# Edge scans set one at a time between a sort's comparisons, and a node search that only counts the keys below

## What is computed

```
edge_index = stack([src, dst]); x = layernorm(x + L0(x, edge_weight)); x = layernorm(x + L1(x, edge_attr_64)) ...
L0: col = dst;  geo_agg = x + segment_sum(w * x[col], col) / segment_sum(w, col);  two matmuls with relu
L1: agg_sum = segment_sum(edge_attr, dst); agg_max = segment_max(edge_attr, dst); cnt = segment_sum(1, dst)
    h = gelu([x, agg_sum, agg_max, agg_mean, u[batch]] @ W1 + b1) @ W2 + b2; layernorm; + x
L2: h = relu([x[src], x[dst]] @ W1 + b1); inter = h @ W2 + b2; gated = inter * sigmoid(inter @ Wg + bg)
    pooled = segment_sum(gated, src) / max(segment_sum(1, src), 1)
L3: attention over the edges of each dst (segment max, exp, segment sums of x[src] * alpha)
```

## Time and profile before

| | us |
|---|---|
| median of 3 runs (lowest, highest) | 5547.71 (5546.32, 5547.77) |
| the profiled execution: its time | 5548.05 |
| its span in the trace | 5546.3 |
| sort stage: scans on the DVE (388 full ones) | 476.2 |
| sort stage: comparisons and signs on the DVE | 420.7 |

### The profile page before, as it was taken

One profiled execution on the slowest core, in us unless ns is written; L12 is line 12 of the kernel. 1 busy time (PEld: TensorE's weight loads), 2 busy tenths in 40 slices (PEclk: granted clock), 3 DMA queues, 4 the chain that ended last, 5 costly groups with the idle time before them and its releaser, 6 DMA issues. The chain is left out here.

```text
span 5546.3 us, 56323 instructions
## 1 busy us (share of the span) xinstructions
PE 3195.1 (58%) x11758; PEld 1912.6 (34%) x11758; DVE 3739.0 (67%) x4499; ACT 1742.1 (31%) x3305; POOL 3549.1 (64%) x3650
## 2 busy tenths in 40 slices
PE   4666766274555555555555542666666676666661
PEld 2444444132333333333333322333333343333330
DVE  8998988683333333333333343888888888888886
ACT  2334444162111111111111111444444444444441
POOL 5244000656777777777777767777777777777773
PEclk8667777586777777777677765777777777777775
DMA  8876665463444444444444422444444444444441
GB/s 185 208 230 194 219 189 160 133 135 96 118 119 119 119 119 119 116 116 119 118 119 119 119 68 60 100 104 103 104 103 104 104 104 103 104 104 104 103 93 31
DMA packets 995252, 677.18 MB, mean 122 GB/s; under 512 B 645759, under 2 KB 799123, under 8 KB 994258
## 3 DMA queue, kind: packets, MB, share of 16 engines
q1 hardware_dynamic: 719604, 344.35, 25.3%
q0 software_dynamic: 116160, 120.60, 12.2%
q10 hardware_dynamic: 159390, 211.24, 10.7%
HBM read 343.26 MB, written 332.55 MB: 122 GB/s over the span
## 5 line engine op out<-in xcount | busy, mean ns | idle before, releaser
L1570 POOL DMA_INDIRECT got<-tabg,ix x1568 | 1479.3, 943 | 489.1 <-issue 477.6
L1763 POOL DMA_INDIRECT got<-tabg,ix x1568 | 1479.4, 943 | 477.7 <-issue 477.7
L177 PE MATMUL p_got<-ident,got 128*128 128x128 f32 (+1 forms) x784 | 208.0, 417 | 910.5 <-DMA got<-tabg,ix 910.5
L1684 DVE TENSOR_TENSOR pre<-own,p_got 128x512 f32<-128x512 f32 x196 | 134.4, 686 | 877.7 <-PE p_got L177 794.3
L184 PEld LDWEIGHTS p_out<-ident,run 128*128 128x128 f32 (+1 forms) x3136 | 532.1, 215 | 311.8 <-issue 304.2
L184 PE MATMUL p_out<-ident,run 128*128 128x128 f32 (+1 forms) x3136 | 625.0, 347 | 5.4 <-DVE run L1948 3.5
L1796 PE MATMUL p_got<-ident,got 128*128 128x128 f32 (+1 forms) x784 | 177.3, 366 | 654.0 <-DMA got<-tabg,ix 654.0
L1637 ACT ACTIVATE hid<-pre,B 128x512 f32<-128x512 f32 x196 | 141.2, 720 | 1278.7 <-DVE pre L1684 1278.7
L532 DVE TENSOR_TENSOR_SCAN run<-p_mk,run,feat 128x512 f32<-128x512 f32 x390 | 477.2, 1266 | 79.1 <-ACT feat L637 42.9
L177 PEld LDWEIGHTS p_got<-ident,got 128*128 128x128 f32 (+1 forms) x784 | 133.3, 208 | 958.9 <-DMA got<-tabg,ix 958.9
L1668 DVE TENSOR_TENSOR_SCAN own<-mk,own,p_first 128x512 f32<-128x512 bf16 x195 | 248.6, 1275 | 298.9 <-PE p_first L177 298.9
(11 more groups left out here) (358 smaller groups left out, 6641.9 us busy)
## 6 DMA issues: line engine op xcount, KB each, us to landing
t<-rows ACTq DMA_DIRECT2D x195, 512.0 KB
first<-start SPq DMA_DIRECT2D x390, 256.0 KB
t<-rows ACTq DMA_DIRECT2D x195, 288.0 KB, 2.3
got<-tabg,ix POOLq DMA_INDIRECT x3136
start<-zeros SPq DMA_DIRECT2D x100, 500.0 KB
ea<-in_ea_dram SPq DMA_DIRECT2D x390, 128.0 KB
mk<-marks SPq DMA_DIRECT2D x780, 64.0 KB, 2.7
start<-zeros SPq DMA_DIRECT2D x195, 256.0 KB
```

The lines of the kernel that those rows point to most:

```text
L177: mm = nc.tensor.transpose(by_place(bank, g)[:, :, cc], by_edges[0:g.p, cc, :, :].rearrange("p h f -> p (h f)"), ident[0:g.p, 0:g.p])
L1570: nc.gpsimd.indirect_dma_start(got[s][0:g.p, cc, h, :], None, tabg, bass.IndirectOffsetOnAxis(ap=ix[0:g.p, g.n, h, cc:cc + 1], axis=0)).th ...
L1763: nc.gpsimd.indirect_dma_start(got[s][0:g.p, cc, h, :], None, tabg, bass.IndirectOffsetOnAxis(ap=ix[0:g.p, g.n, h, cc:cc + 1], axis=0)).th ...
```

## The change

1. **Placement.** `scans_beside` counts 392 single scans. A scan comes after single comparison instructions, in proportion to their columns (1.14 scans per 1024 columns); a turn takes four scans, and before these one more where needed so that they begin with a sum (5 of the 12 turns that still have scans). The scans left when the last 32 steps begin, eight of them, all stand after the first instruction of that stretch.
2. **PE and ACT.** Work goes in entries, one per scan. An entry m (group n, kind) on the PE is: one mark matmul for that kind, waiting only for the scan of the same kind of group n-1; `p_out` of that scan; in a sum's entry also `p_in` of group n+1. In a turn the third entry stands between the second and third quarter of the keys. The marks have a semaphore per kind. All is written out, without loops.
3. **Search.** `count_keys` makes only the keys below; `has` and `first` are made once for all 49 columns by `find`, in tick 17, from `upto` (the next node's `before`). The carried column is issued by SP ahead of the table stores, and the scatter waits for `find`.

```
 def scans_beside(steps):
-    rate = (NG + 1 - 2 * turns) / (last - turns)
...
-        if what[0] == "turn":
-            k = 2
...
+    rate, credit, at, out = (SCANS - (IN_TURN + 1) * turns) / work, 0.0, 0, []
...
+        if i >= busy:
+            out.append([take(SCANS)])
+        elif what[0] == "turn":
+            out.append([take(at % 2), take(IN_TURN)])
+        else:
+            n, w = ops_of(what)
...
+            for _ in range(n):
+                credit += rate * w
...
 SP load
-                    wait_from(sp, spread, g.n - AHEAD + 1)
+                    wait_from(sp, marked_maxima, g.n - AHEAD + 1)
 DVE scan
-                    dve.wait_ge(spread, g.n + 1)
-                    dve.wait_ge(feats, g.n + 1)
-                    wait_from(dve, rowed, 2 * g.n - 2)
+                    dve.wait_ge(spread[kind], g.n + 1)
+                    if kind == 0:
+                        dve.wait_ge(feats, g.n + 1)
+                    wait_from(dve, rowed, m - 3)
 PE
+                def spread_marks(g, kind):
+                    wait_from(pe, scanned[kind], g.n)
+                    nc.tensor.matmul(p_mk[kind][:, 0:g.w], sel2[:, :], mk[g.slot(AHEAD)][:, kind, 0:g.w], start=True, stop=True).then_inc(spread[kind], 1)
+                def entry(m):
+                    n, kind = m // 2, m % 2
...
+                        spread_marks(Group(None, n), kind)
+                    if n > 0:
+                        turn_back(Group(None, n - 1), kind)
+                    if kind == 0 and n + 1 <= NG:
+                        turn_group(Group(None, n + 1))
 turn_keys
                     for q in range(4):
+                        if q == 2 and m < SCANS + 2:
+                            entry(m)
+                            m += 1
 ACT entry
+                    if kind == 1 and n + 1 <= NG:
+                        to_order(Group(None, n + 1))
+                    if n > 0:
+                        to_rows(Group(None, n - 1), kind)
 count_keys
-        nc.vector.tensor_tensor(self.upto_it[:, 0:k, :], keys, node, ALU.is_le).then_inc(self.v, 1)
...
+        self.link(dve, nc.vector.tensor_tensor(self.less[:, 0:k, :], keys, node, ALU.is_lt))
+        self.link(dve, nc.vector.tensor_reduce(self.count1[:, s], self.less[:, 0:k, :], AX.X, ALU.add))
+        nc.vector.scalar_tensor_tensor(out=self.before[:, s], in0=self.row[:, s], scalar=float(SORTED_KEYS), in1=self.count1[:, s],
+                                       op0=ALU.mult, op1=ALU.add).then_inc(self.counted, 1)
 SP of node_chain
+                if firsts_of:
+                    firsts_of.shift(sp)
                 for u, (a, k) in enumerate(UNITS):
...
-                if firsts_of:
-                    firsts_of.shift(sp)
 POOL of node_chain
-                        pool.wait_ge(firsts_of.found, u + 1)
+                        pool.wait_ge(firsts_of.found, 1)
```

More of the change, by code:

```diff
@@ L391, in mark_rows, with ops_of, take @@
     yield slice(E // SF, E // SF + 1), slice(0, E % SF), marks[1, kind, E // SF * SF - H:H].rearrange("(o f) -> o f", o=1)
-def scans_beside(steps):
-    last = len(steps) - QUIET
-    turns = sum(1 for what in steps[:last] if what[0] == "turn")
-    rate = (NG + 1 - 2 * turns) / (last - turns)
-    out, n, credit = [], 0, 0.0
+SCANS = 2 * (NG + 1)
+IN_TURN = 4
+def ops_of(what):
+    if what[0] == "sign":
+        return 1, SF // 2
+    return (4, SF // 4) if what[1] < ROW else (2, SF // 2)
+def scans_beside(steps):
+    busy = len(steps) - QUIET
+    turns = sum(1 for what in steps[:busy] if what[0] == "turn")
+    work = sum(n * w for n, w in (ops_of(what) for what in steps[:busy] if what[0] != "turn"))
+    rate, credit, at, out = (SCANS - (IN_TURN + 1) * turns) / work, 0.0, 0, []
+    def take(k):
+        nonlocal at
+        k = min(k, SCANS - at)
+        at += k
+        return range(at - k, at)
     for i, what in enumerate(steps):
-        if what[0] == "turn":
-            k = 2
-        else:
[L405 to L411, removed]
+        if i >= busy:
+            out.append([take(SCANS)])
+        elif what[0] == "turn":
+            out.append([take(at % 2), take(IN_TURN)])
+        else:
+            n, w = ops_of(what)
+            after = []
+            for _ in range(n):
+                credit += rate * w
+                k = int(credit)
+                credit -= k
+                after.append(take(k))
+            out.append(after)
     return out
@@ L424, in sort_and_edge_sums @@
     beside = scans_beside(steps)
-    ticks_of_turns = [beside[i].start if beside[i] else NG + 1 for i in turns_at]
+    scans_of_turns = [beside[i][-1].start for i in turns_at]
     with Stage(nc) as c:
@@ L544, in _, with scan_on @@
                 for i, what in enumerate(steps):
+                    scans = iter(beside[i])
+                    def scan_on():
+                        for m in next(scans, ()):
+                            scan(m)
                     if what[0] == "turn":
                         turns += 1
-                        for n in beside[i]:
-                            scan(Group(None, n))
+                        scan_on()
+                        scan_on()
                         if turns == CLEAR_TURN:
@@ L906, in fetch_keys @@
         pool.wait_ge(self.rows_counted, u + 1)
-        wait_from(pool, self.found, u - 2)
+        wait_from(pool, self.counted, u - 2)
         for j in range(a, a + k):
```

147 lines of the change are left out of this document (74 added, 73 removed).

## The result

The changed kernel takes 5509.9 us, median of four runs (5509.45 to 5513.84), against 5547.0 for the kernel before in the same comparison: ratio 0.9932, 95% interval 0.9921 to 0.9944. The forecast was 5503, with 5480 to 5535 as its range. The profiled execution of the changed kernel is its slowest run (5513.84, span 5512.1, 34.2 under the span of before). The gain sits where the change is: the VectorE's first instruction behind the sort stage moved from 1068.16 to 1043.22 (24.9 earlier, 33.8 forecast), and the first gather of the edge stage behind `node_chain` from 1325.83 to 1290.60, so the third stage became 10.3 shorter (10.7 forecast). Behind that point the difference stays between 34.2 and 35.3 us.

The account below looks back on a forecast made before the run. The sort was taken as bound by the DVE's own work plus waits, falling from 79.1 to 45.3 us. That gain of 33.8 plus 10.7 from the search made 44.5, giving 5503 us, range 5480 to 5535.

Parts of the forecast that it names:

- Ordinary waits: Sort, between turns: the twenty ordinary DVE waits for marks go, since each scan waits for its own kind's marks: -19.1 us.
- Turns: Sort, twelve turns: DVE waits fall to 28 us from 53.4, mean 2.3 per turn, bounds 15 and 52.
- low at the start and high from the second half on: PE clock case at a sort turn: lower level first, upper from the second half, some 3.4 us of waits per turn.
- The rival with the lower clock through the whole turn: PE stays at the lower clock at sort turns: turns cost 52, last scans 7, time 5531; chance 0.12.
- Loads: Sort: loads have 15.4 us to land instead of 17.7, so waits behind late ones rise from 6.6 to 8.9 us.
- term (a): Sort step ends: 23 steps no longer end in a scan, so dependent instructions follow directly, 0.18 each: 4.1 us added.
- (b): Sort start: the first scan stands after two comparisons, not four, and its features come about 1.3 us late.
- (c): Sort end: the eight last scans stand in a row and wait for the PE, 1 to 7 us, taken as 3.
- The search: Third stage: five units from tick 12 save 2.1 us each, so the stage end moves by 10.7; bounds 6 and 12.
- search's gain hidden: Rival, third stage: the search's gain is hidden by ACT or POOL, time 5508 to 5514; chance 0.1.
- waits only move: Rival, sort: each single scan has its own PE handshake; at 0.25 for each of 332 scans, time 5586; chance 0.04.
- loads become the bound: Rival, sort: late loads block marks on the PE; 0.5 us more for each of 196 groups gives 5601; chance 0.05.

Follow-up runs that it names:

- Experiment 11: Changed kernel with scans put back in pairs or fours at step ends, marks and turns still per kind: 5534.4 us, ratio to before 0.9977.
- experiment 6: Changed kernel with the marks of a turn's fourth and fifth scans ahead of the first and second half of the keys: 5504.7 us, ratio to before 0.9924.
- experiment 5: Changed kernel with every mark matmul issued twice: 5627.6 us, ratio to before 1.0148.
- Experiments 7: Changed kernel with three more unused comparisons of keys with nodes in each of the first seven search units: 5513.7 us, ratio to before 0.9935.
- experiment 8: Changed kernel with three more unused comparisons of keys with nodes in each of search units 8 to 12: 5522.5 us, ratio to before 0.9957.
- experiment 4: Changed kernel without the PE's entry between the two halves of the keys at a turn: ratio to before 0.9932, in a comparison with long pauses.
- Experiment 12: Changed kernel with fourth scan's marks between key halves, fifth's behind, sums and features last, and six load slots for four: ratio to before 0.9883, with long pauses.

## Why the prediction was right, and where it was off

**Ordinary waits (-19.1): right.** No scan between turns waits, but for three behind late loads. Experiment 11 brings 17 such waits back by the placement alone.

**Turns (28 forecast, 40.7 measured): the term that was mis-sized.** The walk's clocks held: the case "low at the start and high from the second half on" is what the turns show, it was put at 3.4, and the mean of the twelve was 3.4. That the two agree so closely is in part luck, since the walk had two waits per turn, and nine turns have a third ahead of the keys. What failed is the step "I take half the turns at 1.25 and half at 3.4", taken from the median key transpose of before. Before, eight of the twelve turns were entered at the upper clock. In the changed kernel all twelve are entered at the lower clock. The rival with the lower clock through the whole turn was off too, since the second half of the keys ran at the upper level in all twelve; but the keys don't bring that level by themselves, as experiment 6 and seven turns of experiment 5 show. Experiments 7 and 8 have the same sort, and their turns cost 38.2 each, so the 40.7 of the one profile is on the high side. Experiment 5 says how tight the PE is, experiment 4 that its order at the turn is worth 0.9 per turn.

**Loads (8.9): right**, 4.61, 0.29 and 3.79, together 8.7; in experiments 7 and 8, with the same sort, 10.1 each. Experiment 12 shows that more slots shorten them.

**Step ends, term (a), 4.1.** A comparison that needs the one just before it, and one that has a scan between:

```profile
302.41 0.67 DVE L595 TENSOR_TENSOR kb<-ka 128x512 f32<-128x512 f32 x1
303.12 0.69 DVE L595 TENSOR_TENSOR ka<-kb 128x512 f32<-128x512 f32 x1
...
304.92 0.67 DVE L595 TENSOR_TENSOR ka<-kb 128x512 f32<-128x512 f32 x1
305.50 1.28 DVE L557 TENSOR_TENSOR_SCAN run<-p_mk,run,feat 128x512 f32<-128x512 f32 x1
```

The next instruction follows after 0.71 where it depends and after 0.58 where it doesn't: 0.13, so 23 of them are 3.0. The rule of the Trainium skill, VectorE: DVE Perf Modes, section "The DRAIN you can't avoid", would make it 0; this case's rows do not agree. **(b)**, 1.3, did not happen: the first scan started at 54.28 with no wait. **(c)**, 3: the last eight scans waited 2.75. The PE's need of 3.8 us per group at the lower clock was put a little low; it is 4.0.

**The sum for the sort.** Waits of 39.9 were forecast and 52.1 came, 12.2 more, nearly all at turns; (a) and (b) were 5.4 and are about 2 by the balance (waits fell by 27.0, the stage by 24.9). So 33.8 became 24.9.

**The search (10.7): right**, 10.3, and experiments 7 and 8 confirm both halves of the argument. POOL's last work moved by 10.3 against the stage's start, as forecast; its first scatter by 6.2, where I said 8.

**The rivals.** The rival "search's gain hidden" gave 5508 to 5514, and the result lies in it, but by another way: the third stage did shrink by 10.3 and experiment 8 shows its price; what is missing was lost at the turns. That waits only move did not come true at the time's scale, though experiment 6 shows it in small: waits that leave the marks return on the keys. That loads become the bound did not come true either.

## What to carry to other kernels

Where one engine is full and another feeds it, spreading the consumer's items evenly removes the waits that come from two in a row; here the kernel with pairs was 24.5 us slower than the one with even scans, while the finer semaphores and the split turn alone made the sort 2.5 us shorter. But count the feeder's work at its lower clock before calling it slack: here that is 4.03 of 4.62 us per item, and 0.86 more made it the bound. When a forecast rests on how fast an engine ran before, ask whether the change alters the order of its work.

## What was not expected of the hardware

The PE's clock fell with the same matmuls in another order (0.76 to 0.62 granted, and the stretch above), and didn't rise when more was added: busy 195 of 200 us and granted 0.57, in experiment 5. It is not the even placement of the scans that does it. Experiment 11 has the scans in pairs as before and only the new entries on the PE, and its clock is as low:

```profile
420.00:940.00 520.00, 439.62 (x1796) 286.46 (x1796) 468.87 (x409) 223.08 (x390) 56.93 (x51) 0.63 0.64 198
```

So the fall came with what else changed in the sort, the entries written out for PE and ACT: the PE makes one mark matmul and four transposes at a time in place of two and eight. Which part of that does it, no run shows. The prediction gave "evenly fed it may fall" as the reason of its lower-clock rival; the fall came with pairs of scans too. The Trainium skill, TensorE: Matmul & The Clock Gate, section "What's actually happening", has recent activity release the full clock; here the stretch of before, with the clock at 0.76, has the smallest busy share of the three (370 of 540 us, against 464 of 520 and 195 of 200). Part of that is effect and not cause, since the same mark matmul takes 0.60 us at the lower clock and 0.39 at the upper. What does decide it stays open.

The issue of one group's loads, 1.22 us as a rule, took the SyncE 16.68 us once, and the wait of 4.61 behind it is the largest of the sort. The trace of before has the same at the same place, 18.09 us from 73.49 on. The rows of the changed kernel:

```profile
73.20 16.68 SPq L495 DMA_DIRECT2D ea<-in_ea_dram  x2
...
93.94 1.28 DVE L557 TENSOR_TENSOR_SCAN run<-p_mk,run,feat 128x512 f32<-128x512 f32 x1 [4.61 <-PE p_mk L637]
```
